# The second product for the mixing weights on rows 32 to 39 of the array

## The chip, the cores and the metric

One core of a Trainium2 chip. The metric is the device time of one execution in microseconds; the number of a kernel is the median of its runs. The profile beside it is of one execution, whose own time is given with it.

## The reference, cut to what matters

x has 128 samples of 32 channels by 512. Two layers follow each other, each adding its result to x. The first layer mixes the channels of each sample with weights of its own, made from a condition, and sends the result through a feed-forward layer with experts; the second does a grouped convolution and another feed-forward layer with experts.

```python
att   = softmax(mlp(cond))                        # 128 samples x 8 kernels
agg_w = einsum('bk,koi->boi', att, weight)        # mixing weights: 128 x 32 x 32
agg_b = att @ bias_k
y     = einsum('boi,bih->boh', agg_w, x) + agg_b[:, :, None]
x     = x + (y @ W_up.T + lora_of_the_best_expert(y))
c     = conv1d(x, w, groups=4) + ctx + fside
x     = x + (c @ W_base.T + b_base + lora_of_the_two_best_experts(c))
```

The change is in how `agg_w` is computed. It is a product with a contraction of only 8 (the kernels) for 128 samples and 32 x 32 = 1024 columns.

## The kernel before, in words

The 128 x 32 rows of x are worked on in 32 tiles of 128 rows (four samples each). Each engine runs its own program; semaphores order them. A body is called for the steps 0 to 33, the first four and the last four written out, the others as a loop over pairs. In step i, TensorE computes the first layer's up product for tile i, the convolution and the base product for tile i - 1, and the mix for tile i + 1.

Before and during the first two steps the weights are prepared. fp32r operands are split into a high part (ACT copies, `high_part`) and a low part (VectorE subtracts, `low_part`) after TensorE has transposed them (`fill(n)`, 13 of them; each has a PSUM bank and may have to wait until that is free). The condition goes through a small network; its softmax `att` is transposed to `attT` (8 x 128) on VectorE (L750), then `att_b` is made (L762), from which POOL makes `prod` (L427), VectorE the sums `gsum` (L689) and the blocks `mix_w` (L697) with which the first three tiles are mixed.

The later tiles take their mixing weights from two products at the end of step 0 (L1226). Their stationary operand is `attT`, their moving operands are the two halves of `wk_s`, the 8 kernels with 1024 columns; the first goes to the bank ps_turn, the second to ps_conv. ACT copies the first to `mix_b` (L648), VectorE the second (L953), in the order of their queues: ACT after moving rows of tile 0 and making a high part, VectorE after the low part of it. Both count up mixb_ready. For that wait SP, which stores mix_b to DRAM, in step 1 reads it back as blocks into `mix_all` and then, in its queue, moves the rows of tile 1 (`move_x`) for the convolution; and TensorE in step 1, ahead of its next fills (L1184), since one of them takes ps_conv.

`y_sum` (L711) adds the bias to a mixed tile on VectorE, ACT makes `y_hi` (L573), POOL `y_lo`. The up product (`first_up` for tile 0, `up_half` for the others) begins with y_hi (L1028, L1154) and ends with y_lo (L1033, L1164). VectorE picks the expert (gl, zm), TensorE turns z, and x1 is y's result plus x.

`wk_s` is loaded by SP as one DMA (L350) just before the base weights (L333), which POOL reorders into `base_p` (L451) for the fills.

Of the kernel before, what the change touches and what calls it, by code (L numbers as in the profile page):

```python
# [12 lines left out]
P = 128  # L13
B = 128
C = 32
H = 512
# [8 lines left out]
KATT = 8  # L25
# [20 lines left out]
def adaln_ffn(nc, x, cond, fside, W0, b0, W1, b1, W2, b2, wmix, bias_k, w_up, gate_w,  # L46
# [7 lines left out]
    with ExitStack() as ctx:  # L54
        def sb(name, shape, dt=F32):
            return ctx.enter_context(nc.sbuf_tensor(name, shape, dt))

        def sem(name):
            return ctx.enter_context(nc.semaphore(name))

        def bank(name, banks=1):
# [30 lines left out]
        att, attT = sb("att", [P, KATT]), sb("attT", [KATT, P])  # L92
# [26 lines left out]
        xt = sb("xt", [P, 2, H])  # L119
        prod, gsum = sb("prod", [P, C, KATT]), sb("gsum", [P, C])  # L120
        mix_w = sb("mix_w", [P, SPT, C])
        wk_s, mix_b = sb("wk_s", [KATT, C * C]), sb("mix_b", [B, C, C])
        mix_all = sb("mix_all", [P, NT, P])
        xtp = sb("xtp", [P, 2, H])
        beat = sb("beat", [P, 1])
# [17 lines left out]
        in_cond, in_mlp = sem("in_cond"), [sem(f"in_mlp{n}") for n in range(3)]  # L143
        in_mix, in_bias, in_ctx, in_conv = sem("in_mix"), sem("in_bias"), sem("in_ctx"), sem("in_conv")
        in_rows, in_b1, in_ebias = sem("in_rows"), sem("in_b1"), sem("in_ebias")
        ones_ready, attbias_ready, row0_done, row0_ready = (sem("ones_ready"), sem("attbias_ready"),
                                                            sem("row0_done"), sem("row0_ready"))
        in_up, in_base = [sem("in_up0"), sem("in_up1")], [sem("in_base0"), sem("in_base1")]
# [29 lines left out]
        in_wk, mixb_done, mixb_ready, mixb_out, mix_in = (sem("in_wk"), sem("mixb_done"), sem("mixb_ready"),  # L178
                                                          sem("mixb_out"), sem("mix_in"))
# [61 lines left out]
        def once(tile):  # L241

            return not isinstance(tile, int) or 0 <= tile < NT
# [5 lines left out]
        def after(eng, sem, count):  # L249

            if not isinstance(count, int) or count > 0:
                eng.wait_ge(sem, count)
# [28 lines left out]
        def conv_columns(w):  # L281
            return w[:].rearrange("k g b (p o) -> k (b p) g o", p=NP)

        def conv_turns():
            return ps_base[:, 1].rearrange("k (s g o) -> k s g o", s=WIN, g=GP)
# [41 lines left out]
        def _(sp):  # L327
# [3 lines left out]
            def load_base(half):  # L331
                k2 = slice(half * KC // 2, (half + 1) * KC // 2)
                sp.dma_start(wbase_raw[:, k2], w_base.rearrange("(k p) h -> p k h", p=P)[:, k2])\  # L333
                    .then_inc(in_base[half], 16)
# [12 lines left out]
                if half == 0:  # L347
                    load_x(0, 0)
            sp.dma_start(wctx_s[:], wctx).then_inc(in_ctx, 16)
            sp.dma_start(wk_s[:], wmix.rearrange("k o i a -> k (o i a)")).then_inc(in_wk, 16)  # L350
            load_base(0)
            load_base(1)

# [303 lines left out]
        def _(dve):  # L657
# [67 lines left out]
            for g in range(GP):  # L725
# [35 lines left out]
            dve.wait_ge(attb_done, 1)  # L761
            dve.tensor_copy(att_b[:], ps_conv[:, 0, 0:NT * KATT].rearrange("p (t k) -> p t k", k=KATT))\  # L762
                .then_inc(attb_ready, 1)
            dve.wait_ge(convhi_ready, 1)
            dve.tensor_tensor(conv_columns(conv_lo), conv_turns(), conv_columns(conv_hi), ALU.subtract)\
                .then_inc(conv_ready, 1)
# [192 lines left out]
        def _(pe):  # L959
            pe.wait_ge(ident_ready, 1)  # L960

            def fill(n):

                load, blocks, cnt, width, _, _ = fills[n]
                pe.wait_ge(*load)
                if bank_free[n]:
                    pe.wait_ge(*bank_free[n])
                for k, src in enumerate(blocks):
                    rows_in_, cols = src.shape[0], width
                    outp = 3 * Z0 if n == LB_FILL else P  # L970
                    mm = pe.transpose(bank_of[n][0:outp, k * cols:(k + 1) * cols], src,  # L971
                                      ident[0:rows_in_, 0:rows_in_])
                mm.then_inc(fill_done, 1)
# [194 lines left out]
            def body(i, par):  # L1168
                if isinstance(i, int) and i > NT:
                    return  # L1170
                if once(i):

                    pe.wait_ge(yhi_done, i + 1)
                    after(pe, x1_done, i)
                    if isinstance(i, int) and i == 0:
                        first_up()
                    else:
                        up_half(i, 1, slice(HALF, L0W), upgate_done)
                if isinstance(i, int) and i == 1:
                    up_half(i, 0, slice(0, HALF), up_done)  # L1180
                if isinstance(i, int) and i == 0:
                    pe.wait_ge(fill_lo, NF1)
                if isinstance(i, int) and i == 1:
                    pe.wait_ge(mixb_ready, 2)  # L1184
                    for n in range(NF2 - 1, NF):
                        fill(n)
                    pe.wait_ge(fill_lo, NF2)
                    pe.wait_ge(conv_ready, 1)
                    pe.wait_ge(consts_ready, 3)
                if once(i - 1):  # L1190

                    conv(i - 1, 0, turn_hw if once(i - 2) else None)
                    if isinstance(i, int) and i == 1:
                        pe.wait_ge(fill_lo, NF - 1)
                        turn_z(1)
                    conv(i - 1, 1)
                if once(i):
                    if isinstance(i, int) and i == 0:
                        turn_z(i)
                    elif not isinstance(i, int) or i > 1:  # L1200
                        up_half(i, 0, slice(0, HALF), up_done, turn_z)
                    if isinstance(i, int) and i == 0:
                        make_ctx()
                        fill(NF1)
                        fill(NF1 + 1)
                    lora_delta(i)
                if once(i - 2):

                    pe.wait_ge(hthi_done, i - 1)
                    for n, (lhs, w) in enumerate(((hT_hi, b1_hi), (hT_hi, b1_lo), (hT_lo, b1_hi))):  # L1210
                        if n == 2:
                            pe.wait_ge(htlo_done, i - 1)
                        for j in range(2):
                            mm = pe.matmul(ps_base[:, j, 0:HALF], lhs[:], w[:, j * HALF:(j + 1) * HALF],  # L1214
                                           start=False, stop=(n == 2), skip_group_check=True)
                    mm.then_inc(delta_done, 1)
                if once(i + 1):
                    mix(i + 1, 1 - par)
                if isinstance(i, int) and i == 0:

                    fill(NF1 + 2)
                    pe.wait_ge(in_wk, 16)
                    pe.wait_ge(zT_ready, 1)
                    pe.wait_ge(ctx_ready, 1)
                    for half, to in enumerate((ps_turn, ps_conv)):
                        pe.matmul(to[:, 0], attT[:], wk_s[:, half * H:(half + 1) * H], start=True, stop=True)\  # L1226
                            .then_inc(mixb_done, 1)
                if isinstance(i, int) and i == 1:
                    pe.wait_ge(slots_ready, 1)
                if isinstance(i, int) and i == NT:  # L1230
                    last_base()
                elif once(i - 1):

                    for j, width, done in ((0, L1W, basegate_done), (1, HALF, base_done)):
                        if isinstance(i, int) and i == 1 and j == 1:
                            pe.wait_ge(fill_lo, NF)
                        after(pe, out_done, (i - 2) * 2 + 1 + j)
                        for q in range(NQ):
                            if j == 0 and q == 0:
                                pe.wait_ge(chi_done, 2 * i)  # L1240
                            for w in (base_hi, base_lo):
                                pe.matmul(ps_base[:, j, 0:width], c_hi[:, q], w[:, q, j, 0:width],  # L1242
                                          start=(q == 0 and w is base_hi), stop=False, skip_group_check=True)
                        if j == 0:
                            pe.wait_ge(clo_done, 2 * i)
                        for q in range(NQ):
                            mm = pe.matmul(ps_base[:, j, 0:width], c_lo[:, q], base_hi[:, q, j, 0:width],  # L1247
                                           start=False, stop=(q == NQ - 1), skip_group_check=True)
                        mm.then_inc(done, 1)
                if isinstance(i, int) and i == 1:  # L1250
                    pe.wait_ge(y32_done, 3)

            iterate(pe, body)


# [22 lines left out]
```

## Time and profile before

| | |
|---|---|
| median of 3 runs | 360.82 us (360.65 to 361.15) |
| the profiled execution | 360.71 us, span 358.9 us |
| TensorE busy | 349.1 us (97% of the span) |
| VectorE, POOL, ACT busy | 235.8, 195.9, 137.6 us |
| granted TensorE clock | 1.0 throughout |

The span runs from the first to the last instruction; the rest of the execution's time lies around it. A matmul of f32 operands shows as two weight loads (PEld) and two matmuls (PE). In a row of the timeline the bracket at the end tells how long the engine had been idle and what ended it; "issue" is time in which it waited for nothing that the profile shows.

### The profile page before, as it was taken

How to read it: one execution, taken by the hardware profiler on the slowest of the kernel's cores; microseconds unless marked ns; L12 is line 12 of the kernel's file. 1: busy time of each engine (PE TensorE's matmuls, PEld its weight loads, DVE VectorE, ACT ScalarE, POOL GpSimd, SP SyncE). 2: the span in 40 equal slices, each digit the busy share in tenths (PEclk: the TensorE clock that was granted, in tenths of full speed). 3: DMA queues.
4: the chain of work that ended last, by engine and by line, in shares of the span. 5: the costliest groups of instructions: out<-in, count | busy, mean ns of one | idle time of the engine just before them, and what ended most of it. 6: DMA issues, size and time to landing. Idle time of an engine off the chain costs nothing.

```text
span 358.9 us, 9170 instructions
## 1 busy us (share of the span) xinstructions
PE 349.1 (97%) x2607; PEld 342.2 (95%) x2607; DVE 235.8 (66%) x983; ACT 137.6 (38%) x413; POOL 195.9 (55%) x227
## 2 busy tenths in 40 slices
PE   5999999999999999999999999999999999999996
PEld 4878999999999999999999999999999999999985
DVE  5777666767666667666666676676666676766664
ACT  5566333333443333433433343334332433343331
POOL 5588564545665445556664455466644454666440
PEclk9999999999999999999999999999999999999999
DMA  7747854333344432332443333323344333333221
GB/s 159 217 118 183 183 110 108 62 81 78 76 88 88 88 83 53 65 77 75 87 88 88 78 66 58 79 74 85 88 88 88 59 57 81 74 82 61 60 60 60
DMA packets 54238, 31.91 MB, mean 89 GB/s; under 512 B 43661, under 2 KB 44461, under 8 KB 54225
## 3 DMA queue, kind: packets, MB, share of 16 engines
q1 hardware_dynamic: 39344, 27.42, 31.2%
q10 hardware_dynamic: 14608, 3.87, 7.4%
q0 software_dynamic: 272, 0.47, 0.6%
q8 instruction: 6, 0.10, 0.1%
q14 instruction: 8, 0.06, 0.0%
HBM read 14.28 MB, written 8.93 MB: 65 GB/s over the span
## 4 chain that ended last, share of the span: by engine, by line
PE 91%; POOL 2%; DVE 2%; DMA 2%; issue 1%; SPq 1%; ACT 1%; ACTq 0%; POOLq 0%; DVEq 0%
PE ps_base L1242 20%; PE ps_up L1028 17%; PE ps_base L1247 10%; PE ps_up L1033 8%; PE ps_mix L1092 8%; PE ps_mix L1050 6%; PE ps_conv L1050 6%; PE ps_base L1214 6%; PE ps_up L1075 2%; PE ps_turn L1059 1%; PE ps_turn L1067 1%; DMA xq<-x1s 1%; PE ps_base L971 1%; DMA wconv_s<-in_L_cond_weight 1%; SPq L322 1%
## 5 line engine op out<-in xcount | busy, mean ns | idle before, releaser
L508 POOL TENSOR_TENSOR y_lo<-y,y_hi 128x512 fp32r<-128x512 f32 x30 | 38.7, 1291 | 116.6 <-ACT y_hi L573 116.6
L1242 PE MATMUL ps_base<-base_hi,c_hi 128*128 128x392 f32 (+1 forms) x248 | 75.9, 323 | 0.8 <-DVE ot L837 0.5
L1242 PE MATMUL ps_base<-base_lo,c_hi 128*128 128x392 f32 (+1 forms) x248 | 73.0, 311 | 0.0
L1028 PE MATMUL ps_up<-up_hi,y_hi 128*128 128x292 f32 (+1 forms) x248 | 68.9, 301 | 0.0
L1028 PE MATMUL ps_up<-up_lo,y_hi 128*128 128x292 f32 (+1 forms) x248 | 66.8, 290 | 0.0
L483 POOL TENSOR_TENSOR xq_lo<-xq,xq_hi 128x260 fp32r<-128x260 f32 x64 | 47.5, 743 | 24.7 <-ACT xq_hi L555 24.7
L492 POOL TENSOR_TENSOR x1b<-x1s,bbase_s 128x256 f32<-128x256 f32 x64 | 56.8, 913 | 0.0
L555 ACT ACTIVATE xq_hi<-xq 128x260 fp32r<-128x260 f32 x64 | 27.0, 422 | 55.6 <-DMA xq<-x1s 55.6
L1242 PEld LDWEIGHTS ps_base<-base_hi,c_hi 128*128 128x128 f32 x248 | 46.7, 188 | 1.5 <-DVE ot L837 0.7
L1028 PEld LDWEIGHTS ps_up<-up_hi,y_hi 128*128 128x128 f32 x248 | 47.0, 189 | 0.8 <-ACT y_hi L573 0.8
L573 ACT ACTIVATE y_hi<-y 128x512 fp32r<-128x512 f32 x32 | 20.2, 632 | 70.2 <-DVE y L711 66.6
L1028 PEld LDWEIGHTS ps_up<-up_lo,y_hi 128*128 128x128 f32 x248 | 47.0, 189 | 0.0
L1247 PE MATMUL ps_base<-base_hi,c_lo 128*128 128x392 f32 (+1 forms) x248 | 46.9, 311 | 0.0
L1242 PEld LDWEIGHTS ps_base<-base_lo,c_hi 128*128 128x128 f32 x248 | 46.6, 188 | 0.0
L1033 PE MATMUL ps_up<-up_hi,y_lo 128*128 128x292 f32 (+1 forms) x248 | 41.5, 289 | 0.0
L1247 PEld LDWEIGHTS ps_base<-base_hi,c_lo 128*128 128x128 f32 x248 | 39.4, 189 | 0.0
L433 POOL COPY xtp<-xt 128x512 f32<-128x512 f32 x32 | 38.2, 1193 | 0.0
L1033 PEld LDWEIGHTS ps_up<-up_hi,y_lo 128*128 128x128 f32 x248 | 35.3, 188 | 0.2 <-POOL y_lo L508 0.2
L636 ACT ACTIVATE c_hi<-ps_ct 128x256 fp32r<-128x256 f32 x63 | 20.8, 382 | 34.3 <-DVE ps_ct L827 34.3
L568 ACT ACTIVATE c<-ps_conv,biasT 128x64 f32<-128x64 f32 x128 | 29.6, 314 | 3.8 <-PE ps_conv L1050 0.2
L880 DVE TENSOR_TENSOR gl<-ps_up,ebias_s 128x4 f32<-128x4 f32 x32 | 5.2, 163 | 38.6 <-PE ps_up L1033 38.2
L1092 PE MATMUL ps_mix<-mix_all,xt 128*128 (+1 forms) x232 | 30.6, 275 | 0.0
(218 smaller groups left out, 675.3 us busy)
## 6 DMA issues: line engine op xcount, KB each, us to landing
xt<-in_x SPq DMA_DIRECT2D x32, 256.0 KB, 2.6
out_x<-ot SPq DMA_DIRECT2D x31, 256.0 KB, 2.0
xq<-x1s SPq DMA_DIRECT2D x158, 32.5 KB, 2.2
xq<-x1s ACTq DMA_DIRECT2D x96, 32.5 KB, 2.2
rows<-agg_rows SPq DMA_DIRECT2D x2, 597.0 KB, 4.5
wbase_raw<-in_L_ffn_W_base SPq DMA_DIRECT2D x2, 512.0 KB, 7.1
rows<-agg_rows SPq DMA_DIRECT2D x1, 598.0 KB, 5.0
wup_raw<-in_L_ffn_W_up ACTq DMA_DIRECT2D x2, 256.0 KB, 5.4
```

The source lines that it names most:

```text
L433: pool.tensor_copy(xtp[:, par].rearrange("p (j r m) -> p j r m", j=2, r=NQ), columns_of(xt[:, par]))\
L483: pool.tensor_tensor(xq_lo[:, gp], xq[:, gp], xq_hi[:, gp], ALU.subtract)\
L492: pool.tensor_tensor(columns_of(x1b[:, 1 - par])[:, j], shifted(j), columns_of(bbase_s[:])[:, j], ALU.add).then_inc(x1b_done, 1)
L508: pool.tensor_tensor(y_lo[:], y32[:], y_hi[:], ALU.subtract).then_inc(ylo_done, 1)
L555: act.activation(xq_hi[:, gp], xq[:, gp], ACT.Copy).then_inc(xqhi_done, 1)
L568: act.activation(c32[:, 0, cols], ps_of[0][:, 0, cols], ACT.Identity, bias=biasT[:, 0, bass.ds(t * SPT + b, 1)]).then_inc(c32_done, 1)
L1028: pe.matmul(into, y_hi[:, k], w[:, k, cols], start=(k == 0 and w is up_hi), stop=False, skip_group_check=True)
L1033: mm = pe.matmul(into, y_lo[:, k], up_hi[:, k, cols], start=False, stop=(k == KC - 1), skip_group_check=True)
L1050: mm = pe.matmul(ps_of[gp][:, 0, 0:HALF], w[:, gp, part], rhs[:, gp, :, part:part + NB], start=(n == 0 and part == 0), stop=(n == 2 and pa ...
L1092: mm = pe.matmul(ps_mix[:, 0, k * P:(k + 1) * P], xt[:, par, k * P:(k + 1) * P], weights, start=True, stop=True)
L1242: pe.matmul(ps_base[:, j, 0:width], c_hi[:, q], w[:, q, j, 0:width], start=(q == 0 and w is base_hi), stop=False, skip_group_check=True)
L1247: mm = pe.matmul(ps_base[:, j, 0:width], c_lo[:, q], base_hi[:, q, j, 0:width], start=False, stop=(q == NQ - 1), skip_group_check=True)
```

## The change

The tile `wk_s` now has 40 partitions and 512 columns: the first half of the columns lies on partitions 0 to 7, the second half on partitions 32 to 39, each loaded by a DMA of its own. A new tile `att_rows` holds `attT` twice, on the same partitions; two VectorE copies fill it, behind `att_b` and before `conv_lo`. The first product takes both its operands from partitions 0 to 7, the second from 32 to 39. TensorE waits for both loads and both copies before the products.

```diff
-        wk_s, mix_b = sb("wk_s", [KATT, C * C]), sb("mix_b", [B, C, C])
+        wk_s, mix_b = sb("wk_s", [C + KATT, H]), sb("mix_b", [B, C, C])
+        att_rows = sb("att_rows", [C + KATT, P])
...
-            sp.dma_start(wk_s[:], wmix.rearrange("k o i a -> k (o i a)")).then_inc(in_wk, 16)
+            for half in range(2):
+                sp.dma_start(wk_s[half * C:half * C + KATT],
+                             wmix.rearrange("k (h o) i a -> h k (o i a)", h=2)[half]).then_inc(in_wk, 16)
             load_base(0)
             load_base(1)
...
             dve.tensor_copy(att_b[:], ps_conv[:, 0, 0:NT * KATT].rearrange("p (t k) -> p t k", k=KATT))\
                 .then_inc(attb_ready, 1)
+            for half in range(2):
+                dve.tensor_copy(att_rows[half * C:half * C + KATT], attT[:]).then_inc(attrows_ready, 1)
             dve.wait_ge(convhi_ready, 1)
...
-                    pe.wait_ge(in_wk, 16)
+                    pe.wait_ge(in_wk, 32)
+                    pe.wait_ge(attrows_ready, 2)
                     pe.wait_ge(zT_ready, 1)
                     pe.wait_ge(ctx_ready, 1)
                     for half, to in enumerate((ps_turn, ps_conv)):
-                        pe.matmul(to[:, 0], attT[:], wk_s[:, half * H:(half + 1) * H], start=True, stop=True)\
+                        own = slice(half * C, half * C + KATT)
+                        pe.matmul(to[:, 0], att_rows[own], wk_s[own], start=True, stop=True)\
                             .then_inc(mixb_done, 1)
```

## Rows read from the trace of the kernel before

**Rows 1.** Busy time by stage: stretch, length, then busy us of each engine.
```profile
0.00:46.00 46.00, 40.48 (x259) 34.94 (x260) 32.19 (x107) 24.75 (x53) 30.26 (x48) 1.00 0.68 168
46.00:342.00 296.00, 296.00 (x2261) 295.62 (x2260) 195.01 (x841) 108.82 (x348) 161.38 (x174) 1.00 0.36 78
```

**Rows 2.** Timeline, the two products: start, length, engine, line, operation [idle before].
```profile
24.90 0.29 PEld L1226 LDWEIGHTS ps_turn<-wk_s,attT 8*128 8x128 f32 x2 [0.17 <-issue]
...
25.43 0.18 PEld L1226 LDWEIGHTS ps_conv<-wk_s,attT 8*128 8x128 f32 x1 [0.24 <-issue]
...
25.86 1.02 PE L1226 MATMUL ps_conv<-wk_s,attT 8*128 8x512 f32 x2
```

**Rows 3.** Timeline, what stands around and behind the products.
```profile
25.64 0.63 ACT L573 ACTIVATE y_hi<-y 128x512 fp32r<-128x512 f32 x1 [1.56 <-DVE y L711]
...
26.42 1.28 POOL L471 TENSOR_TENSOR y_lo<-y,y_hi 128x512 fp32r<-128x512 f32 x1 [1.39 <-ACT y_hi L573]
26.80 0.19 PEld L1028 LDWEIGHTS ps_up<-up_hi,y_hi 128*128 128x128 f32 x1 [0.76 <-ACT y_hi L573]
...
27.64 0.60 ACT L549 ACTIVATE base_hi<-ps_ct 128x512 fp32r<-128x512 f32 x1 [1.37 <-issue]
...
27.86 0.59 PEld L1033 LDWEIGHTS ps_up<-up_hi,y_lo 128*128 128x128 f32 x4
...
28.88 1.10 DVE L953 COPY mix_b<-ps_conv 128x512 f32<-128x512 f32 x1
...
30.04 0.42 PEld L971 LDWEIGHTS ps_conv<-ident,base_p 128*128 128x128 f32 x4
```

**Rows 4.** Timeline, SP's store of mix_b and TensorE's last gap of the start.
```profile
30.02 0.33 SPq L393 DMA_DIRECT2D agg_mix<-mix_b  x1
...
43.29 0.30 PEld L1050 LDWEIGHTS ps_mix<-xq_lo,conv_hi 128*128 128x128 f32 x2 [0.29 <-POOL xq_lo L483]
```

**Rows 5.** Timeline of VectorE, from conv_lo to the first y.
```profile
12.66 0.68 DVE L765 TENSOR_TENSOR conv_lo<-ps_base,conv_hi 128x512 fp32r<-128x512 f32 x1
13.60 0.48 DVE L689 TENSOR_REDUCE gsum<-prod 128x16 f32<-128x128 f32 x2 [0.25 <-POOL prod L427]
...
14.11 0.23 DVE L697 TENSOR_TENSOR mix_w<-gsum,quad 128x64 f32<-128x64 f32 x1
14.26 0.75 DVE L697 TENSOR_TENSOR mix_w<-gsum,quad 128x64 f32<-128x64 f32 x1
14.93 1.28 DVE L681 TENSOR_TENSOR up_lo<-ps_up,up_hi 128x512 fp32r<-128x512 f32 x2
16.13 0.68 DVE L681 TENSOR_TENSOR up_lo<-ps_base,up_hi 128x512 fp32r<-128x512 f32 x1
16.77 0.69 DVE L711 TENSOR_TENSOR y<-ps_mix,rows 128x512 f32<-128x512 f32 x1
```

**Rows 6.** Timeline of POOL in the same stretch.
```profile
12.84 0.73 POOL L427 TENSOR_TENSOR prod<-wmix_t,att_b 128x256 f32<-128x256 f32 x1 [4.29 <-DVE att_b L762]
...
14.16 0.77 POOL L427 TENSOR_TENSOR prod<-wmix_t,att_b 128x256 f32<-128x256 f32 x1 [0.59 <-DVE gsum L689]
...
15.82 2.43 POOL L451 COPY base_p<-wbase_raw 128x256 f32<-128x256 f32 x4
```

**Rows 7.** Instructions by line: a copy and an operation, ns min/median/max.
```profile
L732 DVE COPY lane_rep<-lane x1: 206/206/206, 6.7 to 6.7; 128x128 f32<-128x128 f32 x1
...
L754 DVE TENSOR_TENSOR att_bias<-attT,biask_s x1: 279/279/279, 9.9 to 9.9; 8x128 f32<-8x128 f32 x1
```

**Rows 8.** Timeline of VectorE in the loop, an instruction that writes from partition 32.
```profile
54.28 0.45 DVE L827 STREAM_TRANSPOSE ps_ct<-c 128x256 f32<-128x256 f32 x1
54.77 0.28 DVE L807 TENSOR_TENSOR zT<-ps_turn,zT 32x128 fp32r<-32x128 f32 x1
```

**Rows 9.** Instructions by line: the loads of the base weights.
```profile
L333 SPq DMA_DIRECT2D wbase_raw<-in_L_ffn_W_base x2: 407/434/460, 6.3 to 6.7; - x2
...
DMA to landing us min/median/max: 6.7/7.1/7.5
```

More of the change, by code:

```diff
@@ L145, in adaln_ffn @@
         in_rows, in_b1, in_ebias = sem("in_rows"), sem("in_b1"), sem("in_ebias")
+        attrows_ready = sem("attrows_ready")
         ones_ready, attbias_ready, row0_done, row0_ready = (sem("ones_ready"), sem("attbias_ready"),
```

## The prediction

> **What bounds the kernel now.** I read the stages first, then the chain of waits back from the products, then the timeline. From 46 to 342 us TensorE is busy in all 296 us; its gaps lie in the first 46 us and in the tail [rows 1]. So a change in the start reaches the end as the shift that it gives to the moment when TensorE stops waiting, and the loop neither adds to it nor absorbs it. Two chains of the start are touched.
>
> The *late chain*, around the products. They run from 24.9 to 26.9 us [rows 2]. Behind them TensorE loads for the second tile's first half (L1028) at 26.80, 0.53 after y_hi is done (25.64 + 0.63 = 26.27), so it isn't y_hi that it waits for by then, but the second product. The low half (L1033) needs y_lo, done at 26.42 + 1.28 = 27.70, and loads at 27.86. Then TensorE comes to L971, the next fill of the base weights, behind line 1184's wait for mixb_ready: it loads at 30.04, 0.06 after VectorE's copy of the second product ends (28.88 + 1.10 = 29.98) [rows 3]. That copy is late because its queue first takes the low part of a base_hi which ACT makes at 27.64, after 1.37 us of issuing DMAs [rows 3]; the product had lain there since 26.9. The same copy releases SP's store of mix_b (30.02), behind which, in SP's queue, stand the moves of the second tile; with them ends TensorE's last gap of the start, at 43.29 [rows 4].
>
> The *early chain*. VectorE's conv_lo is followed by gsum, which waits 0.25 us for POOL's product prod; from gsum on to y (16.77) VectorE has no gap: each up_lo starts 0.60 after the one before ((16.13 - 14.93) / 2), and y stands only 0.04 behind the last one's 0.60 [rows 5]. y makes y_hi, the first up product waits for it, and from there gl, zm, z, x1s, the second y, y_hi at 25.64, ACT's DMAs and the copy at 28.88 follow each other; I find no link with slack. What VectorE loses before 13.60, beyond the 0.25 and the 0.04, comes out at the end.
>
> **The change, part by part.**
>
> *The second product on other rows.* Each product is two loads and two matmuls, which stream 0.43 apart (25.43, 25.86) [rows 2]. No row shows products on different rows of the array at once. Bounds: nothing, if they still queue, and 2 x 0.43 = 0.86 if the second runs wholly beside the first; they are issued first, first, second, second, so if only neighbours overlap one step of four goes, 0.43, which I take. L1028 could then load at 26.37, and y_hi just allows it (26.27 + 0.06). L1033 would stand before y_lo (27.76) in place of 27.86: 0.10 left. L971 would stand before VectorE's copy, which none of this moves: 0.00 left; SP's store waits for the same copy: 0.00. So nothing, 0.43 and 0.86 give one end. With an earlier copy y_lo would still cap the gain at 0.10.
>
> The Trainium skill, "TensorE: Matmul & The Clock Gate", section "Part 3: Packing small matmuls — row/col tiling", has matmuls on different row groups run together, some 4 ns apart. No row here shows it; by it the products end earlier, and the sum stays as above.
>
> *The two VectorE copies of attT, behind att_b and before conv_lo.* This is the part that costs. The trace has no such copy at this place. Three things make the price.
> (a) Length: a copy of 128 elements a partition within SBUF took 206 ns; a two-input operation on 8 x 128 took 279 [rows 7]. I take 0.21.
> (b) Overlap: VectorE's neighbours overlap (up_lo of 0.68 every 0.60). But zT, which writes from partition 32 on, starts 0.04 after the end of the instruction before it (54.28 + 0.45 = 54.73, then 54.77) [rows 8]. The second copy writes from partition 32 on, and conv_lo behind it from 0: I take both as starting 0.03 after their predecessor's end.
> (c) POOL: prod waits for att_b only, so it still starts at 12.84 and takes 0.73. When VectorE's second mix_w, all in SBUF, was issued at 14.26, 0.10 after the next prod had started (14.16), it took 0.75 where the first took 0.23 (14.11), and ended 0.08 after POOL did (15.01 against 14.93) [rows 5, 6]. conv_lo, which reads PSUM, ran beside prod in its usual 0.68.
> Step by step: the first copy starts where conv_lo did, 12.66, and ends at 12.87. prod is there at 12.84. The second copy could start at 12.90, behind prod: by the row of mix_w it ends 0.08 after it, at 13.57 + 0.08 = 13.65. conv_lo at 13.68; gsum 0.60 later, 14.28, in place of 13.60: 0.68 later. y 0.04 less: **0.64 us**. POOL's next prod waits for gsum and moves by the same 0.68, and base_p and the first y_lo with it.
> The low bound: copies that neither meet POOL nor hold each other up, 0.10 to 0.15 each: conv_lo by 12.96, gsum possible at 13.56: 0. If they only go one behind the other, with POOL behind both: second copy to 13.11, prod from there to 13.84, gsum at 13.87: 0.27, less 0.04 is 0.23. The high bound: copies of 0.28, the second behind prod and counted in full, 13.57 + 0.28 = 13.85, conv_lo at 13.88, gsum at 14.48: 0.88, y 0.84. I take 0.64, since mix_w is the nearest row: VectorE within SBUF, issued just behind POOL's start. The margin is thin: prod is ahead by 0.06.
> conv_lo also frees the bank of the fourth fill, whose transposes come second in the eight from 13.8 on, at about 14.6; it would end at 14.36: still in time.
>
> The Trainium skill has a rule behind (c): "SBUF — State Buffer", section "Who interferes with whom", says that VectorE's copies may read through both of its ports, one of which it shares with GpSimd, and that whoever starts first keeps the pair for the whole instruction. The 0.75 against 0.23 agrees; that a copy meets it too no row here shows.
>
> *The load of wk_s in two.* SP issues one more DMA before the base weights, 0.41 to 0.46 us if it is as long as theirs [rows 9]. Those are issued at 6.3 and 6.7 and land 6.7 to 7.5 later, the first by 13.8; POOL reads them only at 15.82, behind its own prod and DMA issue [rows 6, 9]. 2.0 of cover against 0.46. The products want wk_s at 24.9. Cost 0.
>
> *TensorE's waits* (both loads, the copies): asked for at 24.9, met by 14.6. Cost 0.
>
> Sum: 0 + 0.64 + 0 + 0. Against the profiled execution, 360.71 (a span of 358.9 and 1.8 around it), 361.35; against the median of the runs, 360.82 (360.65 to 361.15), 361.46. **I say 361.4.**
>
> **The rivals.** 0.2%, 0.72 us, is about what a measurement of this kernel tells from no change: from 361.54 on it is slower, below 360.10 faster.
>
> 1. *The copies get through before POOL.* prod starts later than it looks, or the second copy isn't held and is issued at 12.76: 0 to 0.23, so 360.8 to 361.05. For: 0.06 us decides. Against: mix_w lost with 0.10. Chance 0.25. This one is not slower.
> 2. *Time gained on TensorE survives*, because L971 is not released by the copy. Against: 0.06 from the one to the other. y_lo's cap of 0.10 off the forecast: 361.3. Chance 0.04. That the products don't overlap at all, so that the change doesn't do what it says, gives the forecast's time; I hold it 0.2 likely, inside the other cases.
> 3. *The second product gets dearer on its new rows.* The step into the first product cost TensorE 0.17 us of idle before its load [rows 2]; if the second pays that too, and again at the way back, TensorE reaches L971 by 0.2 to 0.3 later, and there it has no slack against 29.98. On top of the copies: 361.6 to 361.8, slower. Chance 0.05. The Trainium skill, "TensorEngine Tiling (Array Packing)", section "Tiling Modes", says that a change of tiling mode drains the array and a change of tile within one doesn't: the 0.17 agrees with the first half, no row shows the second, which would speak against this rival.
> 4. *The base weights land late*, pushed back by the split load. It decides from 2.0 us of lateness on and then passes one for one through base_p to y_lo: over 361.6. Against: 32 KB among loads of 512. Chance 0.03.
> 5. What no row shows (the tiles behind wk_s get other addresses): 0.03 faster by over 0.2%, 0.03 slower.
>
> **How the numbers follow.** The forecast holds the remaining 0.57. It lies 0.1 under the bound of 361.54; with 0.64 uncertain by 0.1 and the runs by 0.15, a third of it, 0.19, falls above. Slower: 0.19 + 0.05 + 0.03 + 0.03 = 0.30. Faster: 0.03. Same: 0.38 + 0.25 + 0.04 = 0.67. Range: from 360.85, the low bound of the copies (0, rival 1's low end) and a little more, to their high bound, 360.82 + 0.84, 361.65.
>
> **What would show it.** VectorE: a first copy of about 0.2 us at 12.66, a second of about 0.75 that ends just behind prod, conv_lo at 13.7, gsum at 14.3 waiting for nobody, y at 17.4. From there every row of rows 3 and 4 later by some 0.6, L971 still just behind the copy, TensorE's last gap ending at about 43.9. TensorE: the third matmul of L1226 beginning with the second. Wrong if prod starts behind the second copy (rival 1), if L971 moves otherwise than the copy before it (2, 3), if base_p waits for its load (4), or if the loop's period changes (5).

## The result, and the profile after

The changed kernel takes 362.38 us in the median (361.77 to 363.4, 20 runs), the kernel before 361.04 in the runs beside it (359.78 to 362.16, 20 runs): a ratio of **1.0040, interval 1.0029 to 1.0051**, slower by 0.4%, some 1.45 us. The forecast was 361.4 with a range up to 361.65, and 0.30 for slower. The profiled execution of the changed kernel took 363.22 us (span 361.4), near the top of its runs; the one of before, 360.71, is in the lower part of its own. So the two traces differ by 2.5 us where the medians differ by 1.3, and a size read from one trace is not yet the size of the effect.

Busy time by stage, of the changed kernel, columns as in [rows 1]:
```profile
0.00:46.00 46.00, 37.90 (x235) 32.01 (x236) 30.97 (x102) 23.28 (x47) 27.82 (x46) 1.00 0.72 168
46.00:342.00 296.00, 296.00 (x2263) 295.86 (x2262) 195.82 (x842) 109.09 (x349) 163.08 (x176) 1.00 0.36 78
```
The loop is untouched: TensorE is busy in all 296 us, as in [rows 1]. What the change costs it costs in the first 46 us, in which TensorE got through 235 matmuls where it had got through 259 (busy for 37.90 us in place of 40.48).

Timeline of VectorE, from att_b to the first y, with POOL's prod and TensorE's first mixing products, to lay beside [rows 5, 6]:
```profile
12.57 0.42 DVE L766 COPY att_b<-ps_conv 128x256 f32<-128x256 f32 x1 [1.22 <-PE ps_conv L1023]
12.91 0.98 DVE L769 COPY att_rows<-attT 8x128 f32<-8x128 f32 x2
13.92 0.69 DVE L771 TENSOR_TENSOR conv_lo<-ps_base,conv_hi 128x512 fp32r<-128x512 f32 x1
14.52 0.47 DVE L693 TENSOR_REDUCE gsum<-prod 128x16 f32<-128x128 f32 x2
...
17.04 0.68 DVE L685 TENSOR_TENSOR up_lo<-ps_base,up_hi 128x512 fp32r<-128x512 f32 x1
17.79 0.69 DVE L715 TENSOR_TENSOR y<-ps_mix,rows 128x512 f32<-128x512 f32 x1
...
13.08 0.73 POOL L431 TENSOR_TENSOR prod<-wmix_t,att_b 128x256 f32<-128x256 f32 x1 [3.72 <-DVE att_b L766]
...
16.07 1.62 PE L1098 MATMUL ps_mix<-mix_w,xt 128*128 128x128 f32 x8
```
The same tile, one by one (ns min/median/max):
```profile
L769 DVE COPY att_rows<-attT x2: 204/472/741, 12.9 to 13.1; 8x128 f32<-8x128 f32 x2
```
The first copy took 204 ns. The second, issued just behind prod's start at 13.08, took 741: it ends at 13.89, 0.08 behind prod (13.08 + 0.73 = 13.81). gsum waits for nobody any more. In this execution everything from att_b on is 0.25 later for another reason (att_b itself starts at 12.57, prod at 13.08 in place of 12.84). Without that shift gsum is 0.67 later than in [rows 5] and y 0.77. Of the 0.77, 0.11 arises at the last step: y starts 0.75 behind up_lo (17.04), where it started 0.64 behind it in [rows 5]; TensorE's first mixing products, which it needs, end at 17.69. Where they end earlier, as in e1 below, y is 0.62 later.

Timeline of the changed kernel, the two products and what stands behind them, for [rows 2, 3, 4]:
```profile
25.91 0.18 PEld L1234 LDWEIGHTS ps_turn<-wk_s,att_rows 8*128 8x128 f32 x1 [0.17 <-issue]
25.92 0.18 PEld L1234 LDWEIGHTS ps_conv<-wk_s,att_rows 8*128 8x128 f32 x1
26.02 0.18 PEld L1234 LDWEIGHTS ps_turn<-wk_s,att_rows 8*128 8x128 f32 x1
26.03 0.18 PEld L1234 LDWEIGHTS ps_conv<-wk_s,att_rows 8*128 8x128 f32 x1
...
25.91 0.69 PE L1234 MATMUL ps_turn<-wk_s,att_rows 8*128 8x512 f32 x1
25.92 0.69 PE L1234 MATMUL ps_conv<-wk_s,att_rows 8*128 8x512 f32 x1
26.45 0.59 PE L1234 MATMUL ps_turn<-wk_s,att_rows 8*128 8x512 f32 x1
26.45 0.59 PE L1234 MATMUL ps_conv<-wk_s,att_rows 8*128 8x512 f32 x1
...
26.65 0.63 ACT L577 ACTIVATE y_hi<-y 128x512 fp32r<-128x512 f32 x1 [1.55 <-DVE y L715]
...
27.34 0.19 PEld L1034 LDWEIGHTS ps_up<-up_hi,y_hi 128*128 128x128 f32 x1 [1.12 <-ACT y_hi L577]
...
27.43 1.29 POOL L475 TENSOR_TENSOR y_lo<-y,y_hi 128x512 fp32r<-128x512 f32 x1 [1.39 <-ACT y_hi L577]
...
28.77 0.57 PEld L1039 LDWEIGHTS ps_up<-up_hi,y_lo 128*128 128x128 f32 x4 [0.33 <-POOL y_lo L475]
...
29.89 1.10 DVE L959 COPY mix_b<-ps_conv 128x512 f32<-128x512 f32 x1
...
31.05 0.42 PEld L977 LDWEIGHTS ps_conv<-ident,base_p 128*128 128x128 f32 x4 [0.25 <-DVE mix_b L959]
31.02 0.33 SPq L397 DMA_DIRECT2D agg_mix<-mix_b  x1
...
34.53 2.38 SPq L377 DMA_DIRECT2D mix_all<-agg_mix  x4
...
37.84 3.18 SPq L324 DMA_DIRECT2D xq<-x1s  x5
...
43.62 0.42 ACT L559 ACTIVATE xq_hi<-xq 128x260 fp32r<-128x260 f32 x1 [4.13 <-DMA xq<-x1s]
...
45.24 0.14 PEld L1065 LDWEIGHTS ps_turn<-ident,hw 128*128 128x128 f32 x1 [0.62 <-DVE hw L879]
```
The two products now run entirely beside each other, 10 ns apart and in one step: from 25.91 to 27.04 (26.45 + 0.59), 1.13 us, where before they took 1.98 (24.90 to 26.88, [rows 2]). TensorE has 0.85 us more there and can do nothing with it: the next load waits for y_hi (27.28, loads 27.34), L1039 for y_lo (28.72, loads 28.77), and L977, which was L971 before, still stands 0.06 behind VectorE's copy (30.99). The last gap of the start closes at 45.24, 1.95 later than in [rows 4], and now it is hw that TensorE waits for (the weights of the second layer's two experts, on VectorE), not xq_lo.

### The profile page after: what moved, and what is told of

Read it like the earlier page. It is cut to its first block, busy times and chain, and to the rows that moved or that the text cites. A ratio compares the mean times of both kernels' runs of the same rounds, so it can differ in the third digit from the quotient of the medians.

```text
span 361.4 us, 9174 instructions
## 1 busy us (share of the span) xinstructions
PE 348.9 (97%) x2607; PEld 342.0 (95%) x2607; DVE 237.3 (66%) x985; ACT 137.7 (38%) x413; POOL 196.0 (54%) x227
## 4 chain that ended last, share of the span: by engine, by line
PE 89%; DMA 3%; POOL 2%; DVE 2%; issue 1%; ACT 1%; ACTq 0%; SPq 0%; POOLq 0%; DVEq 0%
PE ps_base L1250 19%; PE ps_up L1034 17%; PE ps_base L1255 10%; PE ps_up L1039 8%; PE ps_mix L1098 8%; PE ps_mix L1056 6%; PE ps_conv L1056 6%; PE ps_base L1220 6%; PE ps_up L1081 2%; DMA xq<-x1s 2%; PE ps_turn L1065 1%; PE ps_turn L1073 1%; DMA wconv_s<-in_L_cond_weight 1%; PE ps_base L977 1%; POOL xtp L437 1%
## 5 line engine op out<-in xcount | busy, mean ns | idle before, releaser
L1039 PE MATMUL ps_up<-up_hi,y_lo 128*128 128x292 f32 (+1 forms) x248 | 41.6, 289 | 0.1
L1039 PEld LDWEIGHTS ps_up<-up_hi,y_lo 128*128 128x128 f32 x248 | 35.2, 188 | 0.4 <-POOL y_lo L475 0.3
```

The costliest lines, as they stand in the source:

```text
L1039: mm = pe.matmul(into, y_lo[:, k], up_hi[:, k, cols], start=False, stop=(k == KC - 1), skip_group_check=True)
```

## The experiments

The kernels ran in five comparisons (e1 to e4, e5 to e7, e8 to e11, e12 to e15, e16 to e18), each beside the kernel before; the ratio is to that, with its 95% interval in brackets. The medians of the kernel before were 360.3 to 361.4 from one comparison to the next, so ratios, not microseconds, are compared.

**The copies alone (e1).** In the kernel before:
```
             dve.tensor_copy(att_b[:], ...).then_inc(attb_ready, 1)
+            for half in range(2):
+                dve.tensor_copy(att_rows[half * C:half * C + KATT], attT[:]).then_inc(attrows_ready, 1)
...
+                    pe.wait_ge(attrows_ready, 2)
```
The products stay as they were; att_rows is read by nobody.

> The kernel before with nothing but the two VectorE copies of attT into a tile that no product reads (TensorE waits for them, as in the change). Copies theory: the second copy ends just behind POOL's prod and takes about 0.74 us, conv_lo starts 1.0 later than before, y 0.75 to 0.8 later, and the time is that of the change, 1.0 to 1.6 us over before. Load theory (the load of wk_s in two delays others) and rows theory (the second product on its own rows costs): no more than the 0.75, the rest of the change's loss missing.

362.34 us, ratio **1.0041 (1.0022 to 1.0061)**: as large as the whole loss, without the change's products. The copies by tile, of e1:
```profile
L767 DVE COPY att_rows<-attT x2: 203/472/742, 12.7 to 13.0; 8x128 f32<-8x128 f32 x2
```
Again 203 and 742 ns. y is at 17.46, 0.69 later than in [rows 5], of which 0.07 is this execution's shift at att_b: 0.62.

**The copies in idle time (e2).** The change, with the loop of two copies in front of the wait for att_b's product, where VectorE idles:
```
+            for half in range(2):
+                dve.tensor_copy(att_rows[half * C:half * C + KATT], attT[:]).then_inc(attrows_ready, 1)
             dve.wait_ge(attb_done, 1)
```

> The change, with its two copies moved ahead of the wait for att_b, where VectorE stood idle for 1.2 us and POOL for 4.3. Copies theory: both copies take about 0.21 us, conv_lo, gsum and y stand where they stood before, and the time is that of before within 0.2% (361.0 where before is 361.0), since the products' 0.87 us on TensorE is swallowed by the wait for mix_b. Rows theory and load theory: the time stays 0.7 us or more above before.

361.89 us, ratio **1.0024 (1.0010 to 1.0038)**. Timeline of VectorE, of e2:
```profile
11.02 0.45 DVE L766 COPY att_rows<-attT 8x128 f32<-8x128 f32 x2
...
13.59 0.48 DVE L693 TENSOR_REDUCE gsum<-prod 128x16 f32<-128x128 f32 x2 [0.26 <-POOL prod L431]
...
16.72 0.68 DVE L715 TENSOR_TENSOR y<-ps_mix,rows 128x512 f32<-128x512 f32 x1
```
By tile, of e2:
```profile
L766 DVE COPY att_rows<-attT x2: 204/210/217, 11.0 to 11.3; 8x128 f32<-8x128 f32 x2
```
The early chain is as before to 0.05 us, and the second copy, with no prod beside it, is as short as the first. Only 0.16% went away, and 0.24% stayed, clear of its interval. So there is a second loss, of a like size or larger, that the prediction didn't have.

**One copy (e4), and copies that POOL doesn't hold up (e5).** e4 leaves the first product on attT and copies once; e5 makes each copy a sum over an axis of length one, at the change's place:
```
-                dve.tensor_copy(att_rows[half * C:half * C + KATT], attT[:]).then_inc(attrows_ready, 1)
+                dve.tensor_reduce(att_rows[half * C:half * C + KATT], attT[:].unsqueeze(2), AX_X, ALU.add)\
+                    .then_inc(attrows_ready, 1)
```

> The change without its first copy: the first product takes attT itself, which already lies on rows 0 to 7, the second its copy on rows 32 to 39. Copies theory, POOL's part: the one copy is issued at about 12.75, before prod's 12.84, takes 0.21, prod starts up to 0.15 later, y is 0.05 to 0.25 later; the time 0 to 0.4 us over before. If it is not POOL but each copy that costs half of the loss: y 0.4 later, 0.7 us over before. If the copy loses to POOL again: as the change.

> The change with its two copies made by a reduction over an axis of length one, in the same place: the same elements move, but not as a copy. POOL theory (a VectorE copy within SBUF and POOL's prod exclude each other, a reduction and prod don't): two instructions of about 0.28 us behind each other, conv_lo at 12.66 + 0.62, gsum 0.25 to 0.3 later, y 0.25 to 0.4 later; 0.3 to 0.8 us faster than the change. Rival (the second one waits because of where it writes, whatever POOL does): the second takes 0.75 again and the time is that of the change.

e4: 361.49 us, 1.0012 (0.9999 to 1.0026), with gsum later by less than 0.1. e5: 361.52 us, 1.0035 (1.0019 to 1.0052). By tile, of e5:
```profile
L769 DVE TENSOR_REDUCE att_rows<-attT x2: 265/270/275, 12.7 to 13.0; 8x128 f32<-8x128 f32 x2
```
Beside the same prod these two took 265 and 275 ns: the copy is held, this sum isn't, though both stay within SBUF. gsum came 0.27 later (13.89, less this execution's shift of 0.02) in place of 0.67; the time hardly followed (1.0035, where the change has 1.0040), though 0.3 to 0.8 us had been expected.

**What the change does besides.** The load of wk_s in two, alone (e3); the kernel before at the changed kernel's tile addresses (e8); e2 at the old addresses (e9); the early copies alone in the kernel before (e10); e9 with both products on rows 32 to 39, one behind the other (e11).

> The kernel before with the load of wk_s in two DMAs (two column halves onto the same 8 partitions), nothing else. Load theory: 0.5 to 1.5 us slower, with the base weights or x landing later. Copies theory: no change, within 0.2%; base_p starts at 15.8 behind POOL's own work.

> The kernel before with every tile behind wk_s at the address that it has in the changed kernel (1,536 bytes lower from mix_all on; wk_s itself at the end, two pads in its place), nothing else. With the copies early, the change was still 0.24% slower although y stood where it stood before; what is left is the addresses, the products on two groups of rows, or the copies as such. Address theory: 0.1 to 0.4% slower than before. Rows theory and copies theory: no change, within 0.15%.

> The change with its copies early and every tile behind wk_s back at the address of the kernel before (wk_s as wide as before, att_rows at the end). Address theory: as before, within 0.15%. Rows theory: still 0.1 to 0.4% slower.

> The kernel before, at its own addresses, with the two early copies into a tile that no product reads. Copies theory: 0.1 to 0.4% slower though they stand in VectorE's idle time. Rows theory and address theory: as before, within 0.15%.

> The change with early copies, at the addresses of before, with both products on rows 32 to 39, so that they run one behind the other again. Rows theory in the form that the overlap costs: as before, within 0.15%, while the kernel with the old addresses and two groups is slower. In the form that rows 32 to 39 cost by themselves: slower too. Address theory: as before, and so is the kernel with two groups.

| kernel | us | ratio (interval) |
|---|---|---|
| e3, load in two | 360.96 | 0.9995 (0.9978 to 1.0011) |
| e8, addresses alone | 360.82 | 0.9997 (0.9981 to 1.0012) |
| e9, e2 at old addresses | 361.56 | 1.0021 (1.0008 to 1.0034) |
| e10, early copies alone | 361.59 | 1.0025 (1.0012 to 1.0038) |
| e11, both on rows 32 to 39 | 361.75 | 1.0020 (1.0006 to 1.0035) |

Timeline of TensorE, the products of e11:
```profile
24.90 1.12 PE L1232 MATMUL ps_turn<-wk_s,att_rows 8*128 8x512 f32 x2
25.86 1.02 PE L1232 MATMUL ps_conv<-wk_s,att_rows 8*128 8x512 f32 x2
```
On one group of rows they run one behind the other, 24.90 to 26.88, as in [rows 2]: the overlap does come from the different rows. No gain and no cost of it shows (e9 and e11 agree, each known to some 0.15%), nor does a cost of the load or of the addresses. The second loss is in all four kernels with early copies so far (e2, e9, e10, e11), even where nobody reads them (e10).

**VectorE's copy of the second product moved ahead (e6, and e7 = e2 with it).** If that copy releases L971 and the store, an earlier one should make the products' gain of use:
```
+                    low_part(NF1 + 2)
-                    low_part(NF1 + 2)
```
(the line goes from ahead of the copy to behind it.)

> The kernel before, with VectorE's copy of the second product taken ahead of its low part of base_hi, in the idle time in front of it. It tests the late chain: if L971 and SP's store wait for that copy, mixb_ready then comes with ACT's copy at 29.3 in place of 29.98, SP stores at 29.4, and the last gap of TensorE's start shrinks: 0.3 to 0.6 us faster than before. Rival: the gap is set by the moved rows' landing or by another wait, and nothing changes (within 0.2%).

> The change with its copies early and with VectorE's copy of the second product ahead of its low part. The products end 0.87 us earlier on TensorE, so VectorE's copy can start earlier; but ACT's copy sets mixb_ready at 29.3 as in the kernel before with the copy first. If the late chain is as told: the same time as that kernel, 0.3 to 0.6 us faster than before. If the rows bring anything by themselves: faster than that kernel.

e6: 361.14 us, 1.0016 (1.0001 to 1.0030). e7: 362.45, 1.0054 (1.0035 to 1.0072). The 0.3 to 0.6 us that were expected to be gained are not there; both are slower, e6 only just clear of its interval. Timeline of SP, of e6:
```profile
28.34 0.61 SPq L390 DMA_DIRECT2D rows<-agg_rows  x1
29.71 0.33 SPq L393 DMA_DIRECT2D agg_mix<-mix_b  x1
34.10 0.94 SPq L373 DMA_DIRECT2D mix_all<-agg_mix  x2
```
The store is issued earlier (29.71, in spite of a first y 0.41 later than in [rows 5]), but the read-back that waits for it comes 4.39 us later, where it came 3.00 later in the kernel before (30.02 to 33.02) and 3.51 in the changed kernel (31.02 to 34.53). So the read-back itself is not earlier but later. e7 repeats it: 4.77 (30.14 to 34.91), where e2 has 3.16 (29.92 to 33.08). The load of rows (597 KB) stands 1.4 us ahead of the store in e6, 2.1 us in the changed kernel (28.94, 31.02). That the store waits for this load's packets was not tried by itself. In e7's profiled execution TensorE's granted clock fell too (windows, same columns as above):
```profile
44.00:48.00 4.00, 3.59 (x19) 3.38 (x18) 2.58 (x14) 1.58 (x7) 3.69 (x5) 0.58 0.48 169
```
0.58 is a mean of the two levels, 1.2 and 2.4 GHz. No other profile shown here has it there, so e7's trace from 44 us on can't be laid beside the others. Its time can: seven of its nine runs kept the clock at 1.0 on average and have a median of 362.27.

**Which instruction makes the second loss.** Each of these four has VectorE's two instructions more and one wait more on TensorE, ahead of the products. e12 has two fills of a spare column at the place of the early copies, e15 twelve, e14 is e2 with ten; e13 has the wait alone, on a semaphore long raised:
```
+                    pe.wait_ge(attT_copied, 1)
                     pe.wait_ge(zT_ready, 1)
```

> The kernel before with two fills of a spare column by VectorE in its idle time ahead of the copy att_b (it waits there from about 11.1 to 12.5 us), and nothing else: no copy, no semaphore, no wait of TensorE. Theory (the rest of the loss goes with the place of the 16 KB packet of the instruction queue, and VectorE's two instructions more bring that packet forward): the packet starts about 1 us earlier than the 39.5 us of before, the first moved rows are made into xq_hi at 41 us or later instead of 40.2, and the time is 0.2 to 0.25% above before (ratio 1.002 to 1.0025). Rival (the copies cost by what they read, write or signal, or by the new wait on TensorE): the packet stays at 39.5 us and the ratio is 1.000.

> The kernel before with one wait more on TensorE ahead of the two products, for a semaphore that has long been raised. Theory (only VectorE's count of instructions moves the packet): ratio 1.000, packet at 39.5 us, xq_hi at 40.2. Rival (TensorE's one instruction more is what the early copies cost): ratio 1.002 to 1.0025 and the packet a us earlier.

> The changed kernel with its two copies ahead of the wait for att_b's product, and ten fills of a spare column by VectorE ahead of them, in idle time. Theory (the place of the packet makes the rest of the loss, so another place gives another time): the packet of the instruction queue moves again by several us, away from 38.4, and the time is not 1.0024 again: about 1.000 if the packet no longer lies in the landing of the first moved rows (36 to 41 us), up to 1.005 if it falls on another transfer that the loop waits for. Rival (the loss has nothing to do with the packet): 1.002 to 1.0025 wherever it lies.

> The kernel before with twelve fills of a spare column by VectorE in its idle time ahead of the copy att_b. Theory: the packet lies where it does in the run with ten fills and the early copies, and the time is that run's within 0.1%. Rival (the copies themselves cost the 0.6 us): 1.000 here and 0.2 to 0.25% more in the run with the copies.

| kernel | us | ratio (interval) |
|---|---|---|
| e12, two fills | 360.25 | 0.9984 (0.9966 to 1.0001) |
| e13, one wait on TensorE | 361.73 | 1.0023 (1.0006 to 1.0041) |
| e14, e2 and ten fills | 361.02 | 0.9999 (0.9983 to 1.0015) |
| e15, twelve fills | 360.44 | 0.9981 (0.9966 to 0.9997) |

The theory on record for e12 to e15, that VectorE's instructions do it, fell; the rival of e13, that TensorE's wait does it, held. e14 goes with neither: it has the wait and loses nothing. Then the wait was taken out of e2 and of the change itself (VectorE writes zT after the copies, so the wait for zT, which stays, covers them), and put eight times into the kernel before:
```
-                    pe.wait_ge(attrows_ready, 2)
```

> The changed kernel with its two copies ahead of the wait for att_b's product, and without TensorE's wait for them: the wait for zT, which VectorE writes after them, covers it. Theory (what is left of the loss with the copies in idle time goes with TensorE's one instruction more): ratio 0.998 to 1.0005. Rival (it goes with the copies, and the wait by itself is a second, separate loss): 1.0024 again.

> The change as it is, its copies behind att_b, but without TensorE's wait for them. Theory (two terms: about 0.7 us from the second copy, which POOL's product holds up, and 0.6 to 0.9 us from TensorE's one instruction more): the first term alone, ratio 1.0015 to 1.002. Rival (the wait adds nothing): 1.004 as with the change.

> The kernel before with eight waits more on TensorE ahead of the two products, all for a semaphore that has long been raised. Theory (one instruction more on TensorE shifts the rest of its program against the packets that bring it; eight shift it otherwise): not eight times the 0.23% of one wait; a ratio anywhere from 0.998 to 1.004, and the packet of the instruction queue at another time than the 39.0 us that it has with one wait. Rival (each wait costs time on TensorE where it stands): the time grows with their number, the products later by eight times what one wait adds, up to 1.018.

| kernel | with the wait | without |
|---|---|---|
| copies early | e2: 1.0024 (1.0010 to 1.0038) | e16: 0.9996 (0.9982 to 1.0010) |
| the change | 1.0040 (1.0029 to 1.0051) | e17: 0.9998 (0.9984 to 1.0012) |
| the kernel before | e13: 1.0023 (1.0006 to 1.0041) | 1 |
| the kernel before, eight waits | e18: 1.0010 (0.9996 to 1.0023) | |

In three pairs the kernel with the wait is 0.23 to 0.42% above the one without. Only e13 was measured in one comparison with its counterpart; e2 and the change didn't run again beside e16 and e17. So these pairs don't rule out that every kernel comes out lower in the comparison of e16 to e18, where eight waits, too, come to 0.10% only. Over all five comparisons the sign is the same: in each, every kernel with the wait has a higher ratio than every edited kernel without it (1.0012 to 1.0041 against 0.9995; 1.0035 and 1.0054 against 1.0016; 1.0020 to 1.0025 against 0.9997; 0.9999 and 1.0023 against 0.9981 and 0.9984; 1.0010 against 0.9996 and 0.9998). So the wait goes with a loss, but not with a fixed one: e4, e14 and e18 have it at 1.0012, 0.9999 and 1.0010, none of them clear of 1. And e17 fits neither its theory nor its rival: with the copies where the change has them, 1.0015 to 1.002 was expected without the wait, and the 0.9998 leaves nothing clear for the copies.

The loss isn't the wait's own duration. Timeline of TensorE's loads, of e13, the last fill ahead of the products, the products, and L971:
```profile
24.47 0.47 PEld L971 LDWEIGHTS ps_ct<-ident,base_p 128*128 128x128 f32 x4
25.11 0.29 PEld L1227 LDWEIGHTS ps_turn<-wk_s,attT 8*128 8x128 f32 x2 [0.17 <-issue]
...
30.26 0.42 PEld L971 LDWEIGHTS ps_conv<-ident,base_p 128*128 128x128 f32 x4
```
and the same fill of the kernel before, whose products begin at 24.90 [rows 2]:
```profile
24.26 0.47 PEld L971 LDWEIGHTS ps_ct<-ident,base_p 128*128 128x128 f32 x4
```
From the fill to the products it is 0.64 us without the wait and with one, and with e18's eight too (24.86 to 25.50); the 0.17 of [rows 2] is unchanged in all three. L971 of e13 is at 30.26, 5.15 after its products began, as in [rows 2, 3] (24.90 to 30.04: 5.14). Up to there the wait costs nothing.

Behind that one thing sets the kernels with the wait apart: the time from the issue of the second tile's moves to their first conversion. Timeline of the kernel before, not among its rows above (SP's moves of x1s into xq; ACT's first conversion, xq_hi):
```profile
36.21 3.19 SPq L322 DMA_DIRECT2D xq<-x1s  x5
...
40.22 0.42 ACT L555 ACTIVATE xq_hi<-xq 128x260 fp32r<-128x260 f32 x1 [1.75 <-DMA xq<-x1s]
```
The same of e13:
```profile
36.82 3.67 SPq L322 DMA_DIRECT2D xq<-x1s  x5
...
42.16 0.42 ACT L555 ACTIVATE xq_hi<-xq 128x260 fp32r<-128x260 f32 x1 [3.47 <-DMA xq<-x1s]
```
of e17, without the wait:
```profile
37.44 3.17 SPq L324 DMA_DIRECT2D xq<-x1s  x5
...
42.23 0.42 ACT L559 ACTIVATE xq_hi<-xq 128x260 fp32r<-128x260 f32 x1 [3.15 <-DMA xq<-x1s]
```
and of e2, with it:
```profile
36.27 3.61 SPq L324 DMA_DIRECT2D xq<-x1s  x5
...
41.35 0.42 ACT L559 ACTIVATE xq_hi<-xq 128x260 fp32r<-128x260 f32 x1 [2.92 <-DMA xq<-x1s]
```
From the first of SP's moves to the first xq_hi: 4.01 us before, 5.34 in e13, 4.79 in e17, 5.08 in e2, 5.78 in the changed kernel. Over the profiles of all 20 kernels: 3.75 to 4.79 in the eight without the wait, 4.93 to 5.78 in the twelve with it. The ranges don't meet. In the changed kernel ACT's e, VectorE's hw and TensorE's load L1065, the new end of its last gap, come behind it.

That this late landing is where the time goes is not shown. In e2's profiled execution the first xq_hi comes at 41.35, 1.13 later than before, and yet that execution took 360.80 us, 0.09 more than the profiled one of before. In e17's it comes 2.01 later, and in its median the kernel is level.

Why one instruction more of TensorE goes with packets of another queue that land a microsecond later, these runs don't settle. DMA by queue from 38 to 41 us (packets, MB, share of the time of 16 engines), of e13:
```profile
q8 instruction: 1, 0.02, 2.2%
```
and of the kernel before:
```profile
q8 instruction: 1, 0.02, 2.1%
```
A queue named instruction moves a packet of 0.02 MB among the moves. The Trainium skill, "Runtime: NRT & Kernel Launch", section "Instruction fetch mechanics", says that an engine's program is streamed in blocks of 16 KiB by DMA, at a cost mostly hidden; the packets here agree with the size. With one instruction more such a block might be asked for at another moment, and so meet the moves differently. But its presence tells nothing: such a packet starts between 38 and 41 us in 18 of the 20 profiles, with the wait and without it, in all but e6 and e12. Nor does it go by TensorE's instructions alone: in e12 two fills on VectorE put it out of that stretch. In e14 it is there, with the late xq_hi and a ratio of 0.9999. So the packet is a candidate and no more.

## Why the prediction was wrong, point by point

- **The products.** The mechanism was right, the size was at its upper bound: the products took 0.85 us less, where 0.43 was taken of nothing to 0.86. It didn't matter, as told: TensorE's next three loads stand 0.06, 0.05 and 0.06 behind y_hi, y_lo and VectorE's copy, so these set the time there and not the products. e11, with the products in series, gives e9's time.
- **The copies.** 0.21 was forecast for the first, 0.75 for the second with an end 0.08 behind prod; the trace has 0.204, 0.741 and 0.08. For y 0.64 was forecast; 0.62 in e1, 0.77 in the changed kernel's execution, with 0.11 of it from the mixing products. Rival 1, copies that get through before POOL, lost; by e5, where nothing holds the two instructions up, gsum would have been 0.27 later. The rule of the Trainium skill, "SBUF — State Buffer", section "Who interferes with whom", agrees with the 741 ns of a copy beside prod and the 217 of the same copy in e2.
- **That the 0.64 comes out in full ("I find no link with slack").** Not borne out. With TensorE's wait the change and e2, and e1 and e10, differ by 0.16%, 0.58 us, which would fit, though neither difference is clear of the intervals. Without the wait e17, with y at 17.43, is level with e16 and with the kernel before, and 0.64 us would be 0.18%, just within what two such intervals leave. A link with slack does stand in the traces: y waits not only for VectorE's queue but for TensorE's mixing products too, and these don't always end at the same time. Timeline of e8, a kernel without any copy of attT (the products took 1.17 us in the kernel before, 15.49 to 16.66):
```profile
15.52 1.85 PE L1094 MATMUL ps_mix<-mix_w,xt 128*128 128x128 f32 x8
...
17.48 0.69 DVE L713 TENSOR_TENSOR y<-ps_mix,rows 128x512 f32<-128x512 f32 x1 [0.64 <-PE ps_mix L1094]
```
y starts 0.11 behind the end of the products here (17.37), and 0.11 behind it in the kernel before (16.66), so the 0.04 that the prediction saw there was this wait already. Of the fifteen profiled kernels that put nothing behind att_b, nine have y at 16.72 to 16.91; in six it waits 0.29 to 0.70 us for these products and stands at 17.18 to 17.59, about where the copies put it (17.46 in e1, 17.43 in e17). So by these rows the copies cost some 0.62 at y in an execution where the products are early, and less or nothing where they are late anyway. How often they are late, and what that takes off the median, was not measured.
- **TensorE's waits: "asked for at 24.9, met by 14.6. Cost 0". This is the step that failed.** As a wait it cost nothing where it stands, as the 0.64 us from fill to products shows. But the kernels with this one instruction more are slower by 0.23 to 0.42% in three pairs, some 0.8 to 1.5 us, which is more than the whole sum; the change without it measures 0.9998. How the instruction does it stays open: the late landing of the second tile's moves goes with it, the loss not in every kernel (e14). With 0.64 for the copies and the 0.8 of e13 for the wait the change would come to 1.44; it measured 1.45. That is luck as far as is known: by the same sum e17 would have to be 0.18% slower than before.
- **Rival 5, "what no row shows", put on addresses, with 0.03.** Addresses cost nothing (e8, e9). But a thing that no row showed did decide, and it had far too little chance (0.03 for slower) and no price. Edits that the trace gives no reason to be worth anything made 1.0023 (one wait) and 0.9981 (a fill of a spare column twelve times over, 0.9966 to 0.9997).
- **The load in two, the new rows (rivals 3 and 4).** Nothing, as forecast: e3 0.9995, and the products' first load pays the same 0.17 as before.
- **The base.** The forecast started from a median of 360.82 of three runs within 0.5 us; 20 runs of the same kernel spread over 2.4 us. In the five comparisons its medians were 360.3 to 361.4, up to 0.15% from that start, where the bound that was to tell slower from same is 0.2%.

No version beats both kernels. e17, the change without its wait, is level with the kernel before; e12 and e15, with fills that do nothing, are at 0.9984 and 0.9981, e15 just clear of its interval.

## What to carry to other kernels

Don't price a wait at nothing because it is met early: at a few tenths of a per cent one instruction more went with a larger loss here than all that the timeline showed. Before a wait is added, see whether one that stands there already covers it, as the wait for zT did here. A VectorE copy within SBUF that started just behind POOL's prod took that instruction's length (741 ns), so it belongs into a gap (0.45 us for two at 11.02, 0.98 at 12.91). Before a delay is carried to the end, look for every engine that the next step waits for, as y did for TensorE, and look in more than one execution. And a gain on an engine whose next three loads wait for others within 0.06 us is no gain: ask what releases the next instruction before counting what the present one saves.

## What had not been expected of the hardware

- Two products on rows 0 to 7 and 32 to 39, issued one after the other and each of two steps, overlapped entirely: all four loads of weights start within 0.12 us (25.91 to 26.03), the matmuls go pairwise together, though in the program the second product stands behind the whole of the first.
- A copy of 8 x 128 took 204 or 741 ns by what POOL did; a sum over an axis of length one did the same work beside prod in 265 to 275.
- One wait instruction on TensorE that holds nothing up went with 0.23% more by itself (1.0006 to 1.0041); eight of them with 0.10%, not clear of nothing (0.9996 to 1.0023).
- Freeing mix_b's store earlier didn't bring its read-back forward: 4.39 us from the one to the other in e6, 3.00 in the kernel before.
- TensorE's first eight mixing matmuls took 1.17 us in the kernel before and 1.85 in e8, begun at 15.49 and 15.52 and with the same shapes. Why, these runs don't show; the profile's windows give a granted clock of 1.00 in both.
